# A graph network's running sums stored to DRAM in 4 KB runs instead of 2 KB runs

## The reference, cut to what matters

```
msg   = relu(h[src] + edge_feature) + 1e-7
m     = msg * t
alpha = softmax of m over the edges of one destination node
agg   = sum over those edges of msg * alpha
out   = MLP(layernorm(...(h + agg)))          # per node, with a residual
```

## Time and profile before

| what | value |
|---|---|
| median of 3 runs | 5210.84 us (5203.7 to 5215.8) |
| the profiled execution's own time | 5190.08 us |
| its span in the profile | 5188.3 us |
| busy: POOL / DVE / PE / ACT | 60% / 55% / 47% / 34% |
| time of DMA packets, SP's queue (q1) | 23.8% of 16 engines |
| time of DMA packets, POOL's queue (q0) | 10.4% of 16 engines |
| stores `sw_rows<-sw_out` | 392 of 512 KB |
| gathers `zsrc<-z_rows` | 3136 |

### The profile page before, as it was taken

One profiled execution on the slowest core, in us unless ns is written; L12 is line 12 of the kernel. 1 busy time (PEld: TensorE's weight loads), 2 busy tenths in 40 slices (PEclk: granted clock), 3 DMA queues, 4 the chain that ended last, 5 costly groups with the idle time before them and its releaser, 6 DMA issues.

```text
span 5188.3 us, 36882 instructions
## 1 busy us (share of the span) xinstructions
PE 2437.5 (47%) x9731; PEld 1698.6 (33%) x9731; DVE 2861.0 (55%) x3666; ACT 1751.9 (34%) x3407; POOL 3104.2 (60%) x3248
## 2 busy tenths in 40 slices
PE   2465666655434444444433444444452444444454
PEld 2354444443323232333222322333231333323233
DVE  3476666766335555555534555555551555555565
ACT  1333333334223333333323333333341333333333
POOL 4666666663566666666356666666626666666651
PEclk8556655667556666666656666666655666666665
DMA  2344444444123333333213333333321333333332
GB/s 62 94 124 122 123 117 118 123 119 148 40 76 102 102 105 100 104 106 100 90 39 92 96 105 105 98 108 102 100 73 40 104 106 99 104 97 104 98 105 68
DMA packets 369056, 508.17 MB, mean 98 GB/s; under 512 B 171775, under 2 KB 177657, under 8 KB 368828
## 3 DMA queue, kind: packets, MB, share of 16 engines
q1 hardware_dynamic: 262222, 395.37, 23.8%
q0 software_dynamic: 103552, 109.52, 10.4%
q10 hardware_dynamic: 3054, 0.71, 0.1%
HBM read 217.93 MB, written 287.39 MB: 97 GB/s over the span
## 4 chain that ended last, share of the span: by engine, by line
another core or an unknown queue 40%; ACT 20%; issue 19%; DVE 10%; PE 9%; DMA 1%; POOL 1%; DVEq 0%; ACTq 0%; SPq 0%; POOLq 0%
ACT sw_out L604 6%; PE pT L782 5%; ACT r L589 3%; DVE S L1096 3%; ACT decay L596 3%; DVE W L1100 2%; ACT pX L592 2%; ACT u L591 2%; ACT pX L598 2%; DVE pX L1098 1%; PE pX L766 1%; PE pX L771 1%; ACT pA L592 1%; DVE M L1081 1%
## 5 line engine op out<-in xcount | busy, mean ns | idle before, releaser
L511 POOL DMA_INDIRECT zsrc<-z_rows,idx_all x3136 | 3007.7, 959 | 1745.2 <-issue 981.0
L782 PE MATMUL pT<-ident,S 128*128 128x128 f32 x1568 | 606.2, 396 | 2255.3 <-DVE W L1100 1307.1
L604 ACT ACTIVATE sw_out<-pT 128x512 f32<-128x512 f32 x784 | 424.9, 594 | 2603.2 <-remote 1798.0
L782 PEld LDWEIGHTS pT<-ident,S 128*128 128x128 f32 x1568 | 338.2, 216 | 2349.5 <-issue 2208.3
L1096 DVE TENSOR_TENSOR_SCAN S<-decay,S,pX 128x512 f32<-128x512 f32 x296 | 378.3, 1278 | 1099.6 <-ACT decay L596 678.4
L766 PE MATMUL pX<-attr_pair,edge_w 128*128 128x512 f32 x592 | 563.0, 1051 | 141.9 <-issue 75.1
L771 PEld LDWEIGHTS pX<-ident,zsrc 128*128 128x128 f32 x2368 | 479.5, 281 | 355.1 <-issue 264.9
L782 PE MATMUL pT<-ident,W 128*128 128x128 f32 x1568 | 579.2, 379 | 0.0
L1081 DVE TENSOR_TENSOR_SCAN M<-pR,M,u 128x512 f32<-128x512 f32 x296 | 376.5, 1272 | 317.4 <-ACT u L591 240.1
L771 PE MATMUL pX<-ident,zsrc 128*128 128x128 f32 x2368 | 460.7, 360 | 75.5 <-DMA zsrc<-z_rows,idx_all 75.5
L1096 DVE TENSOR_TENSOR_SCAN S<-decay,S,pA 128x512 f32<-128x512 f32 x96 | 122.9, 1280 | 635.9 <-ACT decay L596 386.8
(11 more groups left out here) (189 smaller groups left out, 3166.3 us busy)
## 6 DMA issues: line engine op xcount, KB each, us to landing
sw_rows<-sw_out SPq DMA_DIRECT2D x392, 512.0 KB
attr_pair<-attr_cols SPq DMA_DIRECT2D x153, 512.0 KB
zsrc<-z_rows,idx_all POOLq DMA_INDIRECT x3136
max_cols<-M SPq DMA_DIRECT2D x196, 256.0 KB
attr_in<-in_edge_attr_dram SPq DMA_DIRECT2D x196, 128.0 KB
attr_cols<-attr_pair SPq DMA_DIRECT2D x49, 512.0 KB
z_rows<-z SPq DMA_DIRECT2D x25, 125.0 KB
node_sw<-sw_rows,row_idx POOLq DMA_INDIRECT x100
```

Of the source, the lines that this page charges most:

```text
L511: pool.indirect_dma_start(zsrc[c % RING][:, t4, h, :], None, z_rows, bass.IndirectOffsetOnAxis(idx_all[:, h, t4, c:c + 1].bitcast(U32), 0) ...
L604: act.activation(sw_out[c % 2][:, :, 2 * b:2 * b + 2, :, :].rearrange("p h t s c -> p (t s) h c"), pT[b][:, :].rearrange("p (a h c) -> p a ...
L782: last = pe.transpose(pT[b][:, at:at + P], scanned[c % 2][:, t4:CH:SUB], ident[:, :])
```

## The change

The rows of `sw_rows` are put in another order: the four edges of one partition of the lower half, then the four of the upper half, then the next partition. A chunk's 1024 rows are then one block of 512 KB, and each partition of `sw_out` goes to one run of 4 KB. The edge at place i of the lower half has row `i + 4*floor(i/4)`, the one at place j of the upper half has `j + 4*floor(j/4) + 4`. The row numbers for the nodes and for the seam follow this order; the seam's row is a second number of `seam_end`, which SP loads with a second register load.

```diff
             def store_sw(g0, c):
                 sp.wait_ge(back_sb, 2 * g0 + 2 * (c + 1 + PRE))
-                halves = sw_rows[0:2 * HALF, :].rearrange("(h e) c -> h e c", h=2)[:, c * CH:(c + 1) * CH, :]
-                sp.dma_start(halves.rearrange("h (p t) c -> p h (t c)", t=SUB),
-                             sw_out[c % 2][:, :, :, :, :].rearrange("p h t s c -> p h (t s c)")).then_inc(sw_stored[c % 2], 16)
+                sp.dma_start(sw_rows[2 * c * CH:2 * (c + 1) * CH, :].rearrange("(p e) c -> p (e c)", e=2 * SUB),
+                             sw_out[c % 2][:, :, :, :, :].rearrange("p h t s c -> p (h t s c)")).then_inc(sw_stored[c % 2], 16)
...
                     seam_at = sp.value_load(seam_end[0:1, 0:1], min_val=0, max_val=HALF - 1)
+                    seam_row = sp.value_load(seam_end[0:1, 1:2], min_val=0, max_val=2 * HALF - 1)
...
-                seam_row_ap = sw_rows[bass.ds(seam_at + HALF, 1), :].rearrange("o (s c) -> c (o s)", s=2)
+                seam_row_ap = sw_rows[bass.ds(seam_row, 1), :].rearrange("o (s c) -> c (o s)", s=2)
...
+                def quads(out_ap, in_ap):
+                    v.tensor_scalar(out_ap, in_ap, 1.0 / SUB, -(SUB - 1) / (2 * SUB), ALU.mult, ALU.add)
+                    dve.drain()
+                    v.tensor_scalar(out_ap, out_ap, ROUND, None, ALU.add)
+                    dve.drain()
+                    v.tensor_scalar(out_ap, out_ap, -ROUND, float(SUB), ALU.add, ALU.mult)
+                    dve.drain()
...
-                    v.tensor_scalar(seam_end[:, :], seam_f[0:1, :], -float(1 + HALF_AT), None, ALU.add).then_inc(seam_known, 1)
+                    v.tensor_scalar(seam_end[:, 0:1], seam_f[0:1, :], -float(1 + HALF_AT), None, ALU.add)
+                    v.tensor_scalar(seam_j[:, 0:1], seam_f[0:1, :], -float(1 + HALF_AT), None, ALU.add)
+                    dve.drain()
+                    quads(seam_j[:, 1:2], seam_j[:, 0:1])
+                    v.scalar_tensor_tensor(out=seam_end[:, 1:2], in0=seam_j[:, 1:2], scalar=float(SUB), in1=seam_j[:, 0:1],
+                                           op0=ALU.add, op1=ALU.add).then_inc(seam_known, 1)
...
-                    v.tensor_scalar(scr[:, :], scr2[:, :], float(HALF_AT), float(SW_SHIFT), ALU.is_ge, ALU.mult)
-                    dve.drain()
+                    v.tensor_scalar(scr[:, :], scr2[:, :], float(HALF_AT), float(SUB - 2 * HALF_AT), ALU.is_ge, ALU.mult)
+                    quads(quad[:, :], scr2[:, :])
                     v.tensor_tensor(scr[:, :], scr[:, :], scr2[:, :], ALU.add)
+                    dve.drain()
+                    v.tensor_tensor(scr[:, :], scr[:, :], quad[:, :], ALU.add)
                     dve.drain()
```

More of the change, by code:

```diff
@@ L33 @@
 HALF_AT = E - HALF
-assert HALF_AT <= HALF and NCH % 2 == 0
+assert HALF_AT <= HALF and NCH % 2 == 0 and HALF_AT % SUB == 0
 CUT_COL = (HALF_AT - 1) - (NCH - 1) * CH
 assert 0 <= CUT_COL < CH
-SW_SHIFT = HALF - HALF_AT
 NP, NK = 125, 25
@@ L123, in program @@
         has_edges = sb("has_edges", [NP, NK])
-        seam_end = sb("seam_end", [1, 1], I32)
+        seam_end = sb("seam_end", [1, 2], I32)
         seam_fall = sb("seam_fall", [H, 1])
@@ L191, in program @@
         scr2 = sb("scr2", [NP, NK])
+        quad = sb("quad", [NP, NK])
+        seam_j = sb("seam_j", [1, 2])
         seam_col = sb("seam_col", [NP, 1])
@@ L430, in next_layer, with end_layer @@
                         store_sw(g0, c - 2)
-            def end_layer(l, g0, seam_at):
+            def end_layer(l, g0, seam_at, seam_row):
                 store_m(g0, NPAIR - 1)
@@ L452, in end_layer @@
                     store_z(j)
-                return seam_at
-            seam_at = end_layer(0, 0, None)
+                return seam_at, seam_row
+            seam_at, seam_row = end_layer(0, 0, None, None)
             with sp.Fori(1, L) as l:
@@ L458, in _ @@
                 next_layer(g0)
-                end_layer(l, g0, seam_at)
+                end_layer(l, g0, seam_at, seam_row)
             for j, (k0, w) in enumerate(GROUPS):
@@ L1149, in node_ends_3 @@
                     dve.drain()
-                    v.tensor_scalar(scr[:, :], scr2[:, :], float(HALF_AT), float(SW_SHIFT), ALU.is_ge, ALU.mult)
+                    v.tensor_scalar(scr[:, :], scr2[:, :], float(HALF_AT), float(SUB - 2 * HALF_AT), ALU.is_ge, ALU.mult)
+                    quads(quad[:, :], scr2[:, :])
+                    v.tensor_tensor(scr[:, :], scr[:, :], scr2[:, :], ALU.add)
                     dve.drain()
-                    v.tensor_tensor(scr[:, :], scr[:, :], scr2[:, :], ALU.add)
+                    v.tensor_tensor(scr[:, :], scr[:, :], quad[:, :], ALU.add)
                     dve.drain()
```

## The result

The changed kernel takes 5152.62 us (5151.05 to 5154.08), beside 5210.02 us (5203.7 to 5215.8) of the kernel before: a ratio of 0.9888, interval 0.9876 to 0.9900. Forecast was 5211.8 us. The profiled execution took 5154.08 us, its span 5152.2 us; that of before took 5190.08 us (span 5188.3 us), less than any of its other runs, so the two traces show 36.1 us of the 57.4 us between the medians.

What follows compares the result with a forecast made beforehand. Taken as bound by gathers with TensorE's signals over most of a layer, by the ring TensorE, ACT, DVE over its tail. Terms -0.2 + 0 + 1.2 + 0 = +1.0 us gave 5211.8 us, range 5194 to 5227 us.

Steps and rivals of the forecast that it cites:

- 17 us of DMA time are freed: Over 392 stores, 0.70 engine-us saved on each; no gain inside a layer, since nobody waits for the queue there.
- rival A: TensorE's late signals in layers 1 to 3: shifted stores bring all three to the shortest, gaining 15.2 us, 5196.6 us; chance 0.16.
- Rival B: Gathers before POOL's 156 waits queue behind a 4 KB store packet, 0.079 us each: +12.3 us, 5224.1 us; chance 0.14.
- Rival C: The store, its DRAM side one contiguous block, gets to fewer engines; on one, 392 stores need 8190 us; chance 0.01.
- the layer ends: Four places where POOL's node gathers wait for the last store: 0.05 us sooner each, -0.2 us (0 to -0.4).
- The node rows: The 25 gathers a layer by `row_idx`, same 512-byte rows at other addresses: cost 0, bound ±0.4 us.
- SP's second register load: Once, ahead of the seam's reads: another 0.8 us fits in SP's 1.516 us wait for the last store, cost 0.
- VectorE's stretch: `node_ends_3`, once in the first layer: nine more instructions, 2.25 us of work, taken as +1.2 us (0 to +2.3).
- q1's packets: Mark on the store's DMA queue: packets fall by 50176 to about 212000, share from 23.8% to about 23.5%.
- the ACT wait near 1800 and unnamed: Mark ahead of the copy filling `sw_out`: stays near 1800 us, unnamed; falling by hundreds would make the whole reading wrong.

Runs made afterwards that it cites:

- dve_only: The kernel before with the nine more VectorE instructions and SP's second register load, but the old store and row order: 5204.99 us, ratio 0.9998.
- after_again: The changed kernel, unaltered, measured again beside the kernel before on chip C: 5138.95 us, ratio 0.9932.
- store_only: The kernel before with only the new store (128 runs of 4 KB), row numbers for nodes and seam as they were: 5163.11 us, ratio 0.9924.
- tiny_store: The kernel before with the loop's stores in layers 1 to 3 cut to 16 runs of 256 bytes: 5186.97 us, ratio 1.0040.
- half_128x2k: The kernel before, stores of chunks 0 to 95 in layers 1 to 3 writing the lower half alone, 128 runs of 2 KB; chip B: 4378.05 us, ratio 1.0002.
- after_sp_much_later: The changed kernel with eight semaphore increments on SP behind each store in the loop of layers 1 to 3: 5159.56 us, ratio 0.9924.

## Why the prediction was wrong

**The step that failed** is the sentence that 17 us of DMA time are freed "but the queue is 24% busy and nobody waits for it inside a layer", and with it the rating of rival A. It is true that no store is what ACT waits for. It doesn't follow that the store's form can't move those waits. The prediction found that 1800 and 556 us of waits are ended by something unnamed, let go in jumps of many us, and then costed every edit beside them at its own direct length. A system that locks into one rhythm or another answers a small cause by its own step: here 39.7 us over layers 1 to 3, of which 23.2 us are POOL's waits, for a change that saves each store 0.07 us of 16 engines' time (priced at 0.04 us).

**Rival A** had the mechanism in kind (0.16, 5196.6 us) and the sign. Its size was off: it brought three layers to the shortest one seen, 1267.3 us. But the shortest before was itself mixed, 15 threes in 40 intervals. The term is 39.7 us on the traces where it said 15.2. A count of POOL's intervals in the trace of before gives more than that: 26 singles at 2.9 us, 48 twos at 2.75 and 46 threes at 4.34 are 407 us of waits, and the same 260 chunks in threes 376, an estimate of 31 us. The waits fell by 23.2 us; the tail and the short gaps, the other part, neither count would have given. The argument against A, that the gathers keep their pace, was right as a fact (944 ns each in both) and did not bear on it: the pace is kept between the waits, and the waits changed.

**Rival B** (gather packets behind 4 KB ones) is out by its own mark: POOL's unnamed waits rose from 556 to 604.7 us, but in 140 pieces for 156 where it wanted the same count, and with the named ones POOL waits less. **Rival C** is out: the store alone, in a window of 2 us around it, is

```profile
GB/s 0 0 82 492 492 246 573 410 328 573 410 246 655 410 246 655 246 410 573 328 410 492 410 328 573 410 328 164 0 0 0 0 0 0 0 0 0 0 0 0
DMA packets 144, 0.52 MB, mean 262 GB/s; under 512 B 16, under 2 KB 16, under 8 KB 144
...
q1 hardware_dynamic: 144, 0.52, 63.9%
```

144 packets as forecast, 63.9% where the earlier trace rows have 65.3% and the earlier trace rows 67.5%. That is 1.15 engine-us less than before, not 0.70.

**The other terms.** At the layer ends the chain has

```profile
1289.23 2.59 DMA sw_rows<-sw_out
...
1292.91 2.65 DMA seam_sw<-sw_rows
...
5066.71 2.58 DMA sw_rows<-sw_out
```

against 2.74 and 2.73: 0.15 us a layer, -0.6 us over four where I took -0.2 (bound -0.4). The node rows at their new addresses: the end behind the last copy differs by 0.1 us. SP's second register load fits in as said; the loads and the wait behind them are

```profile
L439 SPq TENSOR_LOAD <-seam_end x1: 610/610/610, 1290.4 to 1290.4; - x1
...
L443 SPq EVENT_SEMAPHORE  x1: 479/479/479, 1291.4 to 1291.4; - x1
```

with 0.48 us of the 1.52 us left, where I had said 0.65 to 0.7. VectorE's stretch was forecast 2.2 us longer. Its ends are

```profile
1178.93 0.14 DVE L1147 TENSOR_SCALAR seam_end<-seam_f 1x1 int32<-1x1 f32 x1
...
1183.55 0.19 DVE L1172 TENSOR_SCALAR scr<-scr 125x25 f32<-125x25 f32 x1 [0.54 <-issue]
...
1185.67 0.18 DVE L1178 CAST row_idx<-scr 125x25 int32<-125x25 f32 x1 [0.51 <-issue]
```

so it takes 6.92 us in place of 3.30: 3.6 us more, since the last steps lie 0.7 us apart instead of 0.25. In the chain over the stretch one drain there is

```profile
1183.01 0.49 DVEq L1171
```

and three more behind it take 0.47 to 0.50 us, where the drains just before take 0.03 us; I can't explain it. Layer 0 ends 3.7 us later, but `dve_only`, with the same work, is at 0.9998, so the 3.6 us can't be told in the total.

**Of the marks set beforehand** these came out: q1's packets (212046 for "about 212000"), its share (23.3% for 23.5%), the ACT wait near 1800 and unnamed (1860.1), the layers more alike (5.8 us apart instead of 9.7). The last was A's mark, and here it came out by luck: the layers of `after_again`, the same kernel, are 17.7 us apart and those of `store_only` 11.8, while those of `tiny_store`, which has no gain, are 4.6 us apart. The range, 5194 to 5227 us, held the cases that were priced, and the price of A was the least that a better rhythm might give, not the most.

## What to carry to other kernels

Where waits of hundreds of us are ended by nothing the profile names, count their intervals before costing an edit: a spread of one, two and three units says that a better rhythm may exist, and the waits per unit of each length price it better than the spread between repeats of the loop does. Less work beside such a rhythm can as well be slower: seven lighter or differently cut stores were 0.4 to 0.7% slower here, and one form alone was 0.6 to 1.1% faster. Run such a kernel on more than one chip before keeping the edit for its own sake: where nothing was held, on chip B, four other forms of the store gained nothing, and the edit itself was not tried there.

## What was not expected of the hardware

The same kernel takes 4377.41 us on one chip and 5169.69 to 5210.02 us on the others, 18 to 19% more, with gathers of the same length (959 ns in the trace of before, 965 ns in `half_128x2k` on chip B). On the slow ones TensorE's signals reach ACT and POOL late while POOL issues gathers: 46 us late at the start of a layer, 3.4 us in the cycle shown above, and SP's plain increments take up to 1.4 us each (L432, maximum 1439 ns, in `after_sp_much_later`; no such increments ran on chip B). One more difference lies in the traces: those of the slow chips hold 20068 to 22178 records of semaphore updates each, those of chip B 76112 to 82243. Every time on record belongs to an execution that also has a recorded span and granted clock, so a rival stands untested: that on these chips recording itself takes part in holding the signals back. Then the late signals, and with them the gain, might be less or absent in an execution that isn't recorded. On the fast one ACT is released by the transposes by name each time:

```profile
1500.61 1.08 ACT L608 ACTIVATE sw_out<-pT 128x512 f32<-128x512 f32 x2 [6.05 <-PE pT L786]
...
1510.23 1.08 ACT L608 ACTIVATE sw_out<-pT 128x512 f32<-128x512 f32 x2 [5.63 <-PE pT L786]
...
1520.37 1.08 ACT L608 ACTIVATE sw_out<-pT 128x512 f32<-128x512 f32 x2 [6.15 <-PE pT L786]
```

Issue of a store on SP takes 372 ns for 256 runs, 333 ns for 128 runs from 128 partitions, 466 ns for 64 runs of 4 KB from 64 partitions, and 315 ns for 16 runs of 256 bytes from 16 partitions (medians of SP's timelines). Neither the runs nor the partitions alone order these times.
